# Moving eight score blocks and the cell update's pieces in a differential-attention and recurrent-cell kernel

## What is computed

```python
x = x + attn(layernorm(x))      # 8 heads, each with two query/key sets of width 16
x = x + cell(layernorm(x))
# attn:  q, k = rotary(x @ Wq.T), rotary(x @ Wk.T);  v = x @ Wv.T
#        probs = softmax(q k^T);  diff = probs[:, :, 0] - lam * probs[:, :, 1]
#        out = rms_norm(diff @ v) * (1 - lambda_init); return out @ Wo.T
# cell (a scan over the 16 batches, state c of 1024 x 256):
#        f, i = sigmoid(x wf + c uf + bf), sigmoid(x wi + c ui + bi); g = tanh(x wc + c uc + bc)
#        c = f * c + i * g
#        result: tanh(x wo + c_final uo + bo)
```

## Time and profile before

| What | Value |
|---|---|
| median of 3 runs | 5145.76 us (5145.76 to 5147.62) |
| the profiled execution | 5152.17 us, span 5150.4 us |
| busy: PE, DVE, ACT, POOL | 4892.0 (95%), 3969.7 (77%), 2875.2 (56%), 2933.0 (57%) us |
| score blocks on PE (`L775`) | 4096, idle before them 136.9 us, of which 135.4 until a maximum |
| maxima on DVE (`L1100`) | 4096, 682 ns each, 2586.5 us |
| pair adds on POOL (`L482`) | 2048, 1416 ns each, 2830.7 us |
| granted PE clock, mean | 0.981 |

### The profile page before, as it was taken

The page is one execution under the profiler, slowest core; times in us unless marked ns, Lnnn a source line. Parts: engine busy times, 40 slices in busy tenths (PEclk is TensorE's granted clock), DMA queues, the critical chain, the costliest instruction groups (busy, mean ns, idle before and its releaser), DMA issues.

```text
span 5150.4 us, 67238 instructions
## 1 busy us (share of the span) xinstructions
PE 4892.0 (95%) x24784; PEld 1759.1 (34%) x24784; DVE 3969.7 (77%) x6295; ACT 2875.2 (56%) x5221; POOL 2933.0 (57%) x2134
## 2 busy tenths in 40 slices
PE   6999999999999999999999999999999999999999
PEld 2224242332423333242332424233242333324237
DVE  6877878887787878878888787888878787887526
ACT  1464646656465664646556464665646566463652
POOL 3572736647275673727657373664727567372740
PEclk7899999999999999999999999999999999999999
DMA  6121221303123130222212122130312313022117
GB/s 144 32 56 49 49 64 44 64 38 63 49 46 71 33 72 35 48 70 46 68 33 57 52 46 64 45 63 38 64 49 46 71 33 75 32 46 60 67 50 286
DMA packets 127724, 311.19 MB, mean 60 GB/s; under 512 B 27298, under 2 KB 30499, under 8 KB 113443
## 3 DMA queue, kind: packets, MB, share of 16 engines
q1 hardware_dynamic: 124178, 289.33, 23.7%
q10 hardware_dynamic: 3216, 17.57, 0.9%
HBM read 172.07 MB, written 99.61 MB: 53 GB/s over the span
## 4 chain that ended last, share of the span: by engine, by line
PE 74%; DVE 22%; ACT 3%; issue 1%; DMA 0%; POOL 0%; ACTq 0%; SPq 0%; DVEq 0%; POOLq 0%
PE o_ps L815 15%; PE st L802 14%; PE s_ps L775 14%; PE st L906 13%; DVE neg_max L1100 10%; PE sum_ps L830 7%; PE st L743 3%; PE st L761 3%; DVE swapped L1078 2%; DVE xa L1075 2%; DVE xa L1083 2%; PE st L980 2%; ACT probs L579 1%; DVE xa L1087 1%; PE st L885 1%
## 5 line engine op out<-in xcount | busy, mean ns | idle before, releaser
L482 POOL TENSOR_TENSOR pair_sum<-probs 128x512 f32<-128x512 f32 x2048 | 2830.7, 1416 | 1248.7 <-ACT probs L579 1248.7
L1100 DVE TENSOR_REDUCE neg_max<-s_ps 128x1 f32<-128x512 f32 x4096 | 2586.5, 682 | 762.2 <-PE s_ps L775 759.6
L579 ACT ACTIVATE probs<-st 128x512 f32<-128x512 f32 x4096 | 2152.2, 604 | 999.4 <-PE st L802 963.3
L775 PE MATMUL s_ps<-k_stack,q_stack 96*128 96x512 bf16 x4096 | 1564.3, 390 | 136.9 <-DVE neg_max L1100 135.4
L802 PE MATMUL st<-q_stack,k_stack 99*128 99x512 bf16 x4096 | 1492.4, 385 | 34.0 <-ACT probs L579 15.8
L815 PE MATMUL o_ps<-probs,values 128*32 128x512 f32 x8192 | 1099.5, 609 | 15.0 <-ACT probs L579 11.8
L802 PEld LDWEIGHTS st<-q_stack,k_stack 99*128 99x128 bf16 x4096 | 369.4, 98 | 1346.4 <-ACT probs L579 826.4
L775 PEld LDWEIGHTS s_ps<-k_stack,q_stack 96*128 96x128 bf16 x4096 | 400.3, 98 | 746.2 <-DVE neg_max L1100 418.5
L830 PE MATMUL sum_ps<-pair_sum,ones 128*32 128x512 f32 x4096 | 534.3, 593 | 9.4 <-DVE o_copy L1144 7.6
L906 PE MATMUL st<-pair_sum,weights 128*128 128x512 f32 x768 | 381.9, 594 | 11.8 <-ACT pair_sum L535 11.8
L529 ACT ACTIVATE probs<-st,gate_bias 128x512 f32<-128x512 f32 x192 | 131.6, 686 | 440.0 <-PE st L906 440.0
(11 more groups left out here) (151 smaller groups left out, 3071.4 us busy)
## 6 DMA issues: line engine op xcount, KB each, us to landing
q_stack<-qk_parts SPq DMA_DIRECT2D x384, 128.0 KB, 4.3
k_stack<-qk_parts SPq DMA_DIRECT2D x378, 128.0 KB, 7.0
swapped<-xa SPq DMA_DIRECT2D x128, 256.0 KB, 2.4
qk_parts<-swapped SPq DMA_DIRECT2D x64, 512.0 KB, 2.8
xa<-in_x SPq DMA_DIRECT2D x16, 1024.0 KB, 5.8
qk_parts<-low_part SPq DMA_DIRECT2D x64, 256.0 KB, 3.1
probs<-in_x SPq DMA_DIRECT2D x16, 1024.0 KB, 9.8
x_rows<-probs SPq DMA_DIRECT2D x16, 1024.0 KB, 3.9
```

What stands on the lines that cost most here:

```text
L482: pool.tensor_tensor(pair_sum[q % 2][:, h, :], probs[a % 4][:, h, :], probs[(a + 1) % 4][:, h, :], ALU.add)\
L579: act.activation(probs[kk % 4][:, h, :], st[n % BANKS][:, :], ACT.Exp).then_inc(exp_done, 1)
L775: pe.matmul(s_ps[i % BANKS][:, :], q_stack[g][0:SROWS, s, t * P:(t + 1) * P], k_stack[g][0:SROWS, s, h * HALF:(h + 1) * HALF], start=True, ...
L1100: dve.tensor_reduce(neg_max2[:, at, i % 2:i % 2 + 1], s_ps[i % BANKS][:, :], AX.X, ALU.max, negate=True).then_inc(max_done, 1)
```

## The change

`LATE` and the order around the output projection: three late blocks go beside the values' second half, six beside the output projection's first half, none beside its second half, and three behind the cell parts of gates 1 and 2. VectorE's six maxima stand ahead of all four adds, and its three behind them. `MIDDLE`: eight blocks of unit 2b + 2 go beside the second unit's projection, with their maxima ahead of `finish_sums`; the plan of the second unit starts at block 8. The banks of the score blocks are turned by one, so that the turned maxima stand in a bank that the third block is the first to reuse; only that one waits for `shift_made`. The early blocks beside the first unit's projection are no longer one to a matmul, but 1, 1, 0, 0, 1, 1, 2, 2. `ROPE_WORK` is 2.7 instead of 1.9, and one cast of the second unit stands a step later. The cell update is cut into products and sums.

```diff
@@ -58,17 +58,18 @@
 
 
 
-LATE = (8, 3, 5, 4, 12)
+LATE = (8, 3, 6, 3, 12)
+MIDDLE = 8
 EARLY = (20, 8)
 BEFORE = EARLY[0]
 NEXT_LN, NEXT_QK = 64, 76
 
 ROPE_AT = ({1: 0, 2: 1, 3: 2, 4: 7, 5: 8, 6: 4, 7: 9, 9: 6, 13: 11, 16: 13},
            {5: 0, 6: 1, 7: 2, 8: 7, 9: 8, 10: 4, 12: 9, 13: 6, 16: 11, 20: 13})
-CAST_AT = ({4: 3, 7: 5, 11: 10, 14: 12}, {8: 3, 12: 5, 14: 10, 18: 12})
+CAST_AT = ({4: 3, 7: 5, 11: 10, 14: 12}, {9: 3, 12: 5, 14: 10, 18: 12})
 SUB_ORDER = (0, 2, 4, 6, 1, 3, 5, 7)
 
-ROPE_WORK = 1.9
+ROPE_WORK = 2.7
 WORK = [[(ROPE_WORK if s in at else 0) + (4 if s > 8 and s % 8 == 3 else 0)
          for s in range(STEPS)] for at in ROPE_AT]
 
@@ -91,7 +92,7 @@
 
 
 PLAN0 = score_plan(sum(EARLY), SCORES, 0)
-PLAN1 = score_plan(0, SCORES - sum(LATE), 1)
+PLAN1 = score_plan(MIDDLE, SCORES - sum(LATE), 1)
 NO_PLAN = [range(0)] * STEPS
 
 
@@ -733,7 +734,7 @@
                         for block in itertools.islice(blocks, 2):
                             score(*block)
 
-            def qk(g, b, ab, blocks=iter(()), each=1):
+            def qk(g, b, ab, blocks=iter(()), each=(1,) * 8):
 
                 for X in range(2):
                     for h in range(2):
@@ -743,7 +744,7 @@
                             mm = pe.matmul(bank(i, b, ab), weights[:, W_Q + X, c, g * P:(g + 1) * P],
                                            xt[:, c, h * HALF:(h + 1) * HALF],
                                            start=(c == 0), stop=(c == KC - 1))
-                            for block in itertools.islice(blocks, each):
+                            for block in itertools.islice(blocks, each[4 * X + 2 * h + c]):
                                 score(*block)
                         mm.then_inc(ring_ready, 1)
 
@@ -767,12 +768,15 @@
             def score(u, g, i):
                 s, t, h = SUB_ORDER[i // 16], i % 16 // 2, i % 2
                 if i == 0:
-                    score_start(u)
+                    stacked(u, 0)
+                if i == BANKS - 1 and u > 0:
+
+                    pe.wait_ge(shift_made, u)
                 if i == SCORES // 2:
                     stacked(u, 1)
                 if i >= BANKS:
                     pe.wait_ge(max_done, SCORES * u + (i - BANKS + 1))
-                pe.matmul(s_ps[i % BANKS][:, :], q_stack[g][0:SROWS, s, t * P:(t + 1) * P],
+                pe.matmul(s_ps[(i + 1) % BANKS][:, :], q_stack[g][0:SROWS, s, t * P:(t + 1) * P],
                           k_stack[g][0:SROWS, s, h * HALF:(h + 1) * HALF],
                           start=True, stop=True).then_inc(score_ready, 1)
 
@@ -780,12 +784,6 @@
 
                 pe.wait_ge(stack_in[0][sub], 16 * BLK * (u + 1))
                 pe.wait_ge(stack_in[1][sub], 16 * BLK * (u + 1))
-
-            def score_start(u):
-
-                stacked(u, 0)
-                if not (isinstance(u, int) and u == 0):
-                    pe.wait_ge(shift_made, u)
 
             def turn_max(u):
                 pe.wait_ge(max_all, u + 1)
@@ -856,7 +854,8 @@
                 u = 2 * b
                 if not last:
                     if b > 0:
-                        qk(0, b, ab, ((u + 1, 1, i) for i in range(BEFORE, sum(EARLY))))
+                        qk(0, b, ab, ((u + 1, 1, i) for i in range(BEFORE, sum(EARLY))),
+                           (1, 1, 0, 0, 1, 1, 2, 2))
                     pe.wait_ge(act_out, ab + QK0 + 4)
                 else:
                     for i in range(BEFORE, sum(EARLY)):
@@ -865,7 +864,7 @@
                 attention(u, 0, u + 1, PLAN0)
                 turn_max(u + 1)
                 if not last:
-                    qk(1, b, ab)
+                    qk(1, b, ab, ((u + 2, 0, i) for i in range(MIDDLE)))
                 key_sums(u, 0, 15)
                 if not last:
                     pe.wait_ge(act_out, ab + QK1 + 4)
@@ -888,14 +887,15 @@
                 for i in range(3):
                     mean_square(i)
                 if not last:
-                    rows_out(VAL, W_V, xt, b, ab, js=(2, 3))
+                    rows_out(VAL, W_V, xt, b, ab, js=(2, 3),
+                             beside=(u + 2, 0, itertools.islice(late, LATE[1])))
                 mean_square(3)
 
-                beside = (u + 2, 0, iter(()) if last else itertools.islice(late, sum(LATE[1:4])))
+                beside = (u + 2, 0, iter(()) if last else itertools.islice(late, LATE[2]))
                 pe.wait_ge(at_norm, 4 * b + 2)
                 rows_out(WO, W_O, attn_t, b, ab, js=(0, 1), beside=beside)
                 pe.wait_ge(at_norm, 4 * b + 4)
-                rows_out(WO, W_O, attn_t, b, ab, js=(2, 3), beside=beside)
+                rows_out(WO, W_O, attn_t, b, ab, js=(2, 3))
 
                 early = iter(range(BEFORE))
 
@@ -921,6 +921,9 @@
                 for i in range(BANKS):
                     turn(GATE + i, b, ab)
                     gate_part(i, True, True, False)
+                    if not last:
+                        for n in itertools.islice(late, i):
+                            score(u + 2, 0, n)
                 own = 2 * b + (1 if last else 2)
                 transposes(xn2, ln2_out, b, own, halves=(0,))
                 pe.wait_ge(xt_out, 4 * own + 2)
@@ -954,7 +957,7 @@
                 score(*block)
             transposes(xa, ln1_out, 1, 1, first_scores)
             pe.wait_ge(xt_out, 8)
-            qk(0, 0, act_base(0, False), first_scores, 2)
+            qk(0, 0, act_base(0, False), first_scores, (2,) * 8)
             for block in first_scores:
                 score(*block)
             turn_max(0)
@@ -1097,7 +1100,7 @@
             def maximum(u, i):
                 dve.wait_ge(score_ready, SCORES * u + (i + 1))
                 at = SUB_ORDER[i // 16] * TT + i % 16 // 2
-                dve.tensor_reduce(neg_max2[:, at, i % 2:i % 2 + 1], s_ps[i % BANKS][:, :], AX.X,
+                dve.tensor_reduce(neg_max2[:, at, i % 2:i % 2 + 1], s_ps[(i + 1) % BANKS][:, :], AX.X,
                                   ALU.max, negate=True).then_inc(max_done, 1)
 
             def join_max(u):
@@ -1192,6 +1195,9 @@
                 attention(u, 0, u + 1, PLAN0, None if last else u + 2)
                 join_max(u + 1)
                 split_shift(u + 1)
+                if not last:
+                    for i in range(MIDDLE):
+                        maximum(u + 2, i)
                 finish_sums(u, 0, 3)
                 attention(u + 1, 1, u + 2, NO_PLAN if last else PLAN1,
                           None if last else u + 3)
@@ -1233,8 +1239,7 @@
                         row_stats(x2, t)
                     if j % 2 == 1:
                         half_stats(b, j // 2)
-                    if j == 1:
-                        maxima(u + 2, late, LATE[3])
+                maxima(u + 2, late, LATE[3])
                 normalise_half(b, 1, x2, xn2)
                 if not last:
                     maxima(u + 2, late, LATE[4])
@@ -1243,21 +1248,30 @@
                         dve.wait_ge(x_in, 16 * b + 48)
                         norm_stats(b + 2, xa, -0.5)
                     split_shift(u + 2)
-                cells(b, ab, 0)
-                maxima(u + 3, early, EARLY[0])
-                cells(b, ab, 1)
-
-            def cells(b, ab, h):
-
-
-                dve.wait_ge(act_out, ab + (act_index(GATE) + 6 * h + 6))
                 for m in range(KC):
-                    f, i, a = (gates[m][:, j, :] for j in range(3))
-                    c = cell_t[:, m, h * HALF:(h + 1) * HALF]
-                    dve.tensor_tensor(i, i, a, ALU.mult).then_inc(cell_step, 1)
-                    dve.tensor_tensor(f, f, c, ALU.mult).then_inc(cell_step, 1)
-                    dve.wait_ge(cell_step, 8 * b + (4 * h + 2 * m + 2))
-                    dve.tensor_tensor(c, f, i, ALU.add).then_inc(cell_ready, 1)
+                    cell_products(b, ab, 0, m)
+                for m in range(KC):
+                    cell_sum(b, 0, m)
+                maxima(u + 3, early, 7)
+                cell_products(b, ab, 1, 0)
+                maxima(u + 3, early, EARLY[0] - 7)
+                cell_products(b, ab, 1, 1)
+                for m in range(KC):
+                    cell_sum(b, 1, m)
+
+            def cell_products(b, ab, h, m):
+
+                dve.wait_ge(act_out, ab + (act_index(GATE) + 6 * h + 3 * m + 3))
+                f, i, a = (gates[m][:, j, :] for j in range(3))
+                c = cell_t[:, m, h * HALF:(h + 1) * HALF]
+                dve.tensor_tensor(i, i, a, ALU.mult).then_inc(cell_step, 1)
+                dve.tensor_tensor(f, f, c, ALU.mult).then_inc(cell_step, 1)
+
+            def cell_sum(b, h, m):
+                f, i = (gates[m][:, j, :] for j in range(2))
+                dve.wait_ge(cell_step, 8 * b + (4 * h + 2 * m + 2))
+                dve.tensor_tensor(cell_t[:, m, h * HALF:(h + 1) * HALF], f, i, ALU.add)\
+                   .then_inc(cell_ready, 1)
 
             dve.wait_ge(x_in, 16)
             norm_stats(0, xa)
```

## The result

| | before | after |
|---|---|---|
| time, median of 4 runs | 5146.69 us (5145.76 to 5152.84) | 5122.24 us (5113.73 to 5124.67) |
| profiled execution, span | 5152.17, 5150.4 | 5122.45, 5120.7 |
| granted clock of the span | 0.981 | 0.981 |

The ratio is 0.9947 [0.9935, 0.9959]: 24 us faster, where 25 were forecast. The agreement is better than the reasons deserve: the terms of the two attention stages were far too high, and a loss that I had not foreseen made up for them. A second measurement of the same kernel (experiment 5) found it 39 us faster than before.

The account below looks back on a forecast made before the run. TensorE's work plus its waits for VectorE set the end, with VectorE and GpSimd together bounding rotary steps. Terms -41 - 27 - 1 - 12 + 26 + 6 + 24 = -25 us gave 5127 profiled, 5121 median, range 5085 to 5146.

Parts of the forecast that it names:

- Rival 4: Output projection: wait returns at the adds, six maxima now ahead of the first; 41 us lost, 5162 us; chance 0.08.
- Rival 2: Second unit's start: the 2.11 us wait goes too, with its clock loss (2.5 + 1.3 us, 15 times); 5064; chance 0.04.
- some 0.4: Second unit's attention: gain in us from moving cast 3 off `copy_o`, where GpSimd isn't binding.
- up to 0.9 later: Second unit, step 14: one more rotary operation before GpSimd's sixth pair could delay that pair by up to 0.9 us.
- all but one of the eight were free, so 0.22 comes back: Second unit's steps losing the eight scores moved beside its projection: only 0.22 us returns against their 1.73 us cost.
- the first two scores of a step are free: Attention steps: TensorE would wait for ScalarE's exponentials anyway, so only scores over two cost, 0.22 us each.
- 2.1 us of stall: Second unit's nine rotary steps (5 to 13): 27.34 us, 2.1 of it stall, put down to VectorE and GpSimd.
- Of the 3.0 us stall, GpSimd holds 2.5: First unit's nine rotary steps: GpSimd's twelve pair operations, ending 23.9 us after the start, fix 2.5 us of the stall.
- -0.5 is the best: First unit's attention: the stall can shrink by at most 0.5 us; one more early rotary operation makes +1.0; +0.4 taken.
- rival 1: Rotary steps of both units: VectorE alone holds them, so both stalls go, 89 us less, 5032; chance 0.07.
- One of the two goes. I take half of the losses: Clock: about 1.3 to 1.7 us lost per batch at one of two long waits; removing one wait gives -12 us.
- Rival 3: Both attention units and clock at their bad ends (+1.85, +0.9, clock 0): 5145, no visible change; chance 0.16.

Follow-up runs that it names:

- experiment 5: The changed kernel run once more without an edit: 5108.73 us, 0.9923 of the kernel before.
- experiment 3: Kernel before with only the output projection's new order: 5101.07 us; with only spread early blocks and the cell update in pieces: 5124.99 us.
- experiment 6: e1 with the first unit's last key sums issued inside the second projection: 5032.46 us, 0.9776; the same with the cast at step 9: 5033.35 us.
- e2: Changed kernel with ROPE_WORK 1.9 and the cast back at step 8, MIDDLE staying 8: 5080.17 us, 0.9873 of the kernel before.
- experiment 1: Changed kernel with MIDDLE 0, ROPE_WORK 1.9, cast at step 8: 5080.73 us; the same with MIDDLE 8: 5080.17; changed kernel with MIDDLE 0 alone: 5098.6.
- experiment 4: Rotary operations cut to 64 of 1024 columns, kernel before: 5125.1 us, changed kernel: 5063.44; kernel before with pair adds of 256 of 512 columns: 5125.58.
- e1: Changed kernel without its plan changes (MIDDLE 0, ROPE_WORK 1.9, cast at step 8): 5080.73 us, 0.9874 of the kernel before.

## Why the prediction was right, and where it was not

Sums over the profiled executions, from the starts of the stretches in the trace:

| term | forecast | measured |
|---|---|---|
| output projection | -41 | -39.1 (-2.60 x 15) |
| first unit's projection | -27 | -27.0 |
| cell update of the last batch | -1 | -1.4 |
| clock | -12 | -6.4 (-14.7 at the output projection, +8.3 at the second unit's start) |
| between the units | +26 | +26.4 |
| second unit's attention | +6 | -10.5 (-0.70 x 15) |
| first unit's attention | +24 | +2.3 |
| holds | none | +26.0 |
| sum | -25 | -29.7, as the spans |

- **Output and first projection: right**, in mechanism and size, the adds included; experiment 3 shows each alone. Rival 4, the wait that comes back at the adds, did not happen.
- **Between the units: right.** 1.73 forecast, 1.75 measured, and the wait behind it stayed. Rival 2 (it goes by itself) fell; experiment 6 shows what it takes: an earlier finish of the sums, not fewer scores. What the wait and its clock loss cost, 4.06 us, is near that rival's 3.8; 0.95 of it has to be paid between the units.
- **Second unit: the steps that failed are "some 0.4" for the moved cast and "up to 0.9 later" for the pair.** The kernels with small rotary operations separate the terms. Without rotary work the plan shortens steps 5 to 31 by 0.99 us (86.50 to 85.51). Of this, 0.22 is at step 7 (2.62 to 2.40 us), the only one of them that loses a third score, as "all but one of the eight were free, so 0.22 comes back" has it; my sum, at +1.73, had left this out. The other 0.73 is at steps 9 and 10, and experiment 6 shows it as the moved cast: 0.7 where I took 0.4. What the rotary work adds did move my way, but by 0.29 (0.68 us before, 0.97 after). So the rule that the first two scores of a step are free held in this unit: steps 5 and 6 take 2.41 and 3.27 us with two scores each and no rotary work, and 2.40 and 3.26 us with none in the last batch. It accounts for most of what e2 gained too (experiment 1). What was misread is the "2.1 us of stall": 26.64 is what nine such steps take without rotary work, so 1.4 us of it were the third score (0.22), the cast beside the copy (0.73) and 0.37 at step 13, which both plans have and whose cause stays open.
- **First unit: the step that failed is "Of the 3.0 us stall, GpSimd holds 2.5", and with it "-0.5 is the best".** The plan's own +1.1 is +0.90 (99.57 to 100.47 us without rotary work, experiment 4). The stall fell from 2.71 to 1.95: -0.76 where I took +0.4. I had argued that the pair that the exponentials wait for fixes all behind it. It did come a microsecond later, as forecast: the exponentials that need it start 24.98 us after the unit's start against 23.99 before.

```profile
2325.81 2.06 ACT L580 ACTIVATE probs<-st 128x512 f32<-128x512 f32 x4 [2.32 <-POOL pair_sum L483]
```

  But the steps to 13 end 1.2 us earlier. The lists of waits of these steps (0 to 13, batch 7) show what I had overlooked; before, then after:

```profile
PE s_ps L775 <- DVE neg_max L1100: 1.7, 3, 0.9
ACT probs L579 <- POOL pair_sum L482: 1.2, 2, 1.0
```

```profile
PE s_ps L779 <- DVE neg_max L1103: 0.2, 1, 0.2
ACT probs L580 <- POOL pair_sum L483: 5.1, 4, 2.3
```

  Before, TensorE waited 1.7 us for VectorE's maxima, which stand behind rotary operations; with ROPE_WORK 2.7 these waits are nearly gone, and what is left is GpSimd's pairs. So VectorE's load had a part in the stall, as rival 1 has it, and the plan took that part away. How much of the 0.76 comes from it is my reading of these waits; no run separates the two.
- **A row read wrongly.** The 1.22 us of the second rotary operation of rows 11 are not "elsewhere": it starts at 2357.21 in the middle of a train of pair adds, 0.09 us before the next add, and that add takes 2.27 us instead of 1.27. The first one (2.32 us) starts 0.03 us behind an add of 1.27. So both rows show whose turn it was, and each time the later one paid; the terms do not hang on it.
- **Clock: half right.** The loss at the output projection went whole (14.7 us), but the start of the second unit lost 8.3 us more, in e1 13.2 and in the kernel with the output projection's order alone 4. The step that failed is "One of the two goes. I take half of the losses": part of the loss moves to the wait that is left, and how much differs between the kernels.
- **Missing: the holds.** No term, no rival. Without them this profiled execution would be near 5096, 30 below the 5127 forecast for it. The two units came out 38 us below their terms; 26 of holds, 6 of clock and 2 at the output projection filled most of that. The close agreement is chance. Rival 3 had the right place (GpSimd and the shared port) but not this mechanism. Rival 1 fell: the stalls of the two units went from 2.71 and 0.68 us to 1.95 and 0.97, not to nothing.

**Better than the change:** keep the queue edits, leave MIDDLE and ROPE_WORK, and move the key sums into the projection.

## What to carry to other kernels

When a wait stays after a change, look for what its releaser itself waited for: here eight short matmuls issued 5.2 us earlier were worth 48 us, twice what the whole change gained in its first measurement. When an experiment differs from another in two edits (here the scores and one cast), look at the single steps before you put the difference down to one of them: the time stood in steps whose cast had moved, and not in those whose scores had. And a wait that costs TensorE its clock is worth more than its length, but while another such wait is left, part of that gain can go there.

## What the runs showed of the hardware that I had not expected

- A VectorE operation with two SBUF inputs can be held not by one GpSimd operation but by a train of them: 6.2 us beside the rest of a train at 1.24 us an add, 9.5 us in another, while the same operation of the other batches takes 1.26 to 1.29 us in the first units and 2.01 to 2.15 in the second. The Trainium skill (the section named above) has it that whichever issues first blocks the other for one whole instruction; here one operation is blocked over several. What sets it off stays open: I found no difference in the operations' order or distances.
- The clock's loss is not tied to one wait. The 2.99 us wait brought the lower level in some batches (19.55 us at 0.91) and not in others (17.85 at 1.00) of the same execution; taking up to 51 us of stall away elsewhere made it lose more (25.2 instead of 14.7 us), so that half of the gain was gone.
